# Row numbers for the edge stage's gathers: fetched by SyncE from memory instead of copied by VectorE

## The reference, cut to what matters

```python
xc = x[row]
xn = x[col]
h = relu(xc @ W1[:d] + xn @ W1[d:] + b1)
mask = sigmoid(h @ W2 + b2)[:, 0]
seg_sum = segment_sum(mask, row, num_segments=n)
w = mask / (seg_sum[row] + 1e-09)
agg = segment_sum(w[:, None] * xn, row, num_segments=n)
out_emb = where((deg > 0)[:, None], 0.5 * x + 0.5 * agg, x)
return relu(out_emb @ Wl + bl)
```

## Time and profile before

| | |
|---|---|
| median of three runs | 4384.71 us |
| the profiled execution | 4387.37 us, its span 4385.7 us |
| edge stage, first to last one-hots | 2721.3 to 4281.3 us |
| mean granted TensorE clock | 0.876 |
| busy over the span | PE 82%, DVE 73%, ACT 49%, POOL 35% |

### The profile page before, as it was taken

One profiled execution on the slowest core, in us unless ns is written; L12 is line 12 of the kernel. 1 busy time (PEld: TensorE's weight loads), 2 busy tenths in 40 slices (PEclk: granted clock), 3 DMA queues, 4 the chain that ended last, 5 costly groups with the idle time before them and its releaser, 6 DMA issues. The chain is left out here.

```text
span 4385.7 us, 95324 instructions
## 1 busy us (share of the span) xinstructions
PE 3589.6 (82%) x20539; PEld 2449.5 (56%) x20540; DVE 3189.3 (73%) x13027; ACT 2150.5 (49%) x6722; POOL 1552.8 (35%) x1256
## 2 busy tenths in 40 slices
PE   4868882798889999986997996888888888888884
PEld 2367781333333444433444445777787777777773
DVE  8899997798888888863003006888888888888885
ACT  0078893366767888862002004444444444444444
POOL 0068873000000000001011002776777777777760
PEclk8855555799999999997998998999999999999996
DMA  2011112001111222215874872444444444444451
GB/s 46 1 10 15 16 17 79 18 34 47 68 72 77 93 94 94 102 78 211 304 248 188 305 270 89 140 136 138 136 139 136 139 139 135 140 135 139 137 133 36
DMA packets 236581, 496.86 MB, mean 113 GB/s; under 512 B 52663, under 2 KB 153166, under 8 KB 236350
## 3 DMA queue, kind: packets, MB, share of 16 engines
q1 hardware_dynamic: 170017, 345.58, 23.3%
q0 software_dynamic: 66336, 149.10, 12.5%
HBM read 390.62 MB, written 103.93 MB: 113 GB/s over the span
## 5 line engine op out<-in xcount | busy, mean ns | idle before, releaser
L1676 POOL DMA_INDIRECT xs<-edge_table,ea_row_stage x1088 | 1103.6, 1014 | 463.3 <-issue 307.8
L1842 PE MATMUL ea_psa<-xs,slot_dst 128*128 128x129 f32 x3264 | 456.3, 284 | 239.7 <-DVE agg_t L1756 238.2
L1842 PEld LDWEIGHTS ea_psa<-xs,slot_dst 128*128 128x128 f32 x3264 | 413.7, 194 | 274.0 <-DVE agg_t L1756 265.5
L1231 PE MATMUL a_agg_ps<-a_adj_ring,parts 128*128 128x512 f16 (+1 forms) x2548 | 522.7, 368 | 47.6 <-DMA a_adj_ring<-adjacency 47.5
L1876 ACT ACTIVATE slot_dst<-ea_onehot,ea_mask 128x128 f32<-128x128 f16 x1632 | 535.3, 399 | 13.2
L1030 PE MATMUL ab_agg_ps<-ab_adj_stage,parts 128*128 128x512 f16 x1911 | 532.6, 389 | 0.0
L1756 DVE TENSOR_TENSOR agg_t<-agg_t,ea_psa 128x129 f32 x1632 | 462.9, 284 | 84.3 <-PE ea_psa L1842 69.3
L1870 ACT ACTIVATE ea_mask<-ea_dot,b 128x4 f32<-128x4 f32 x408 | 121.3, 297 | 807.7 <-DVE slot_src L1782 806.3
L448 ACT ACTIVATE dst_step<-iota,dst_low_bias 128x128 f16<-128x128 f16 x1188 | 358.4, 403 | 217.0 <-PEq L473 214.1
L428 POOL DMA_INDIRECT records<-both_parts,record_row x98 | 346.9, 3539 | 313.8 <-ACT both_parts L454 289.5
L1371 POOL TENSOR_TENSOR parts<-xs,parts 128x896 f16<-128x896 f32 x7 | 13.2, 1881 | 1227.9 <-ACT parts L1365 1227.9
(11 more groups left out here) (379 smaller groups left out, 6528.2 us busy)
## 6 DMA issues: line engine op xcount, KB each, us to landing
a_adj_ring<-adjacency SPq DMA_DIRECT2D x182, 896.0 KB, 4.6
ea_low_rows<-low_rows SPq DMA_DIRECT2D x411, 128.0 KB
adjacency<-ab_adj_stage SPq DMA_DIRECT2D x91, 512.0 KB, 2.6
adjacency<-ab_adj_stage SPq DMA_DIRECT2D x91, 384.0 KB, 2.3
ea_near_rows<-near_rows SPq DMA_DIRECT2D x137, 128.0 KB
xs<-edge_table,ea_row_stage POOLq DMA_INDIRECT x1088
edge_table<-vx SPq DMA_DIRECT2D x12, 512.0 KB, 2.9
records<-zero_rows SPq DMA_DIRECT2D x4, 840.0 KB, 10.2
```

The source lines that it names most:

```text
L1231: ins = nc.tensor.matmul(ps[:, h, 0:width], lhs(r, t), ring[:, g % SLOTS, k * DB:k * DB + width], start=t == 0 and r == 0, stop=t == NT - ...
L1676: nc.gpsimd.indirect_dma_start(got[:, h, g, k, 0:ROW], None, m.table, bass.IndirectOffsetOnAxis(ap=row_s[:, h, g, k:k + 1], axis=0)).then_ ...
L1842: ins = nc.tensor.matmul(psa[:, home, k, 0:AW], hot_m[:, g, k, :], what, start=True, stop=True)
```

## The change

The table of row numbers is written once to memory (`row_columns`, 128 x 1664 integers) at the head of the stage. In its step t, SyncE waits until the gathers of pass t have landed, kind by kind, and then fetches the row numbers of pass t+2 into the half of `row_s` that they have left, 128 rows of 16 bytes per kind. GpSimd waits for these DMAs instead of VectorE's copies. A plan row grows by four columns, of which 32 and 33 hold the first columns of pass t+2's far groups; two more DMAs write them in `plan_edges`. VectorE stages the rows of passes 0 and 1 alone.

```diff
@@ plan_edges
+            sp.dma_start(rows_of(0, 32, 34)[:, 0, :], plan[:, 1, 16:18]).then_inc(s_put, 16)
+            sp.dma_start(rows_of(1, 32, 34)[0:TURNS - 1, 0, :], plan[1:TURNS, 0, 16:18]).then_inc(s_put, 16)
-            sp.wait_ge(s_put, 64)
+            sp.wait_ge(s_put, 96)
@@ shared
-    m.plan = nc.dram_tensor("plan_rows", [PLAN_ROWS, 32], I32).ap()
+    m.row_cols = nc.dram_tensor("row_columns", [P, SCP], I32).ap()
+    m.plan = nc.dram_tensor("plan_rows", [PLAN_ROWS, STEP_W], I32).ap()
@@ edge_attention, gpsimd
                 for g in FAR:
-                    gp.wait_ge(s_rows, t * 2 + (g + 1))
-                    if seen >= 2:
+                    if seen < 2:
+                        gp.wait_ge(s_rows, t * 2 + (g + 1))
+                    else:
+                        gp.wait_ge(s_next[h][g], i * 16)
                         gp.wait_ge(s_agg[g], t - 1)
@@ sync
-                base = load(sp, slot, 28, 4)
+                base = load(sp, slot, 28, 6)
...
+            def fetch_next(base, h, i):
+                for g in FAR:
+                    sp.wait_ge(s_got[h][g], i * (16 * G) + 16 * G)
+                    sp.sem_inc(s_seen_sp, 1)
+                    c = nc.s_assert_within(base[g], 0, SC, ...)
+                    sp.dma_start(row_s[:, h, g, :], m.row_cols[:, bass.ds(c, G)]).then_inc(s_next[h][g], 16)
...
-                fetch_rows(1 - h, 1 - h)
+                then = fetch_rows(1 - h, 1 - h)
+                fetch_next(then, h, i)
                 sp.wait_ge(s_read, t + 1)
...
             fetch_rows(0, 0)
-            turns(sp, step)
+            sp.wait_ge(s_table, 1)
+            sp.dma_start(m.row_cols, row_of).then_inc(s_kept, 16)
+            sp.wait_ge(s_kept, 16)
+            turns(sp, step, after=after)
@@ vector
             ch(nc.vector.tensor_scalar(row_of, ai, float(NP - 1), None, ALU.min))
+            dve.sem_inc(s_table, 1)
...
                 base = v[12:15]
-                stage_rows(base, 1 - h)
                 one_hots(base, t, 1 - h, seen)
...
-            base = load(dve, 0, 28, 4)
+            base = load(dve, 0, 28, 6)
             dve.sem_inc(s_read, 1)
-            stage_rows(base, 0)
+            stage_rows(base[0:2], 0)
+            stage_rows(base[4:6], 1)
```

More of the change, by code:

```diff
@@ L36 @@
 PLAN_ROWS = 212
+STEP_W = 36
 ACT_FROM = 5
@@ L770, in plan_edges @@
         plan = sb("plan", [TURNS, 2, 19], I32)
-        none = sb("none", [P, 2 * 32], I32)
+        none = sb("none", [P, 2 * STEP_W], I32)
         psv = ctx.enter_context(nc.psum_tensor("pl_values_ps", [P, NB4, 16], F32))
@@ L1614, in edge_attention @@
         ramp = sb("ramp", [P, P, G], F16)
-        steps = sb("steps", [1, 2, 32], I32)
+        steps = sb("steps", [1, 2, STEP_W], I32)
         row_s = sb("row_stage", [P, 2, 2, G], I32)
@@ L1636, in edge_attention @@
             sem(n) for n in ("v", "ones", "rows", "near_x", "add", "seen", "seen_sp", "seen_dve", "seen_pe", "read", "read_pe"))
+        s_table, s_kept = sem("table"), sem("kept")
+        s_next = [[sem(f"next{h}{g}") for g in FAR] for h in (0, 1)]
         s_hot_t, s_u, s_z, s_dot, s_mask, s_hot, s_hot_m, s_agg = (
@@ L1691, in fetch_rows @@
                 sp.dma_start(rel[:, h, :], m.near_rows[bass.ds(c, G), :].rearrange("(o a) b -> o (a b)", o=1).broadcast_to([P, G * P])).then_inc(s_low[h], 16)
+                return base[4:6]
+            def fetch_next(base, h, i):
+                for g in FAR:
+                    sp.wait_ge(s_got[h][g], i * (16 * G) + 16 * G)
+                    sp.sem_inc(s_seen_sp, 1)
+                    c = nc.s_assert_within(base[g], 0, SC, skip_runtime_bounds_check_because="the plan holds columns")
+                    sp.dma_start(row_s[:, h, g, :], m.row_cols[:, bass.ds(c, G)]).then_inc(s_next[h][g], 16)
             def step(t, h, i, seen):
@@ L1707, in step, with after @@
                 fetch_steps(t + 2, h)
+            def after(end):
+                for h in (0, 1):
+                    for g in FAR:
+                        sp.wait_ge(s_next[h][g], end * 16)
+                        sp.sem_inc(s_seen_sp, 1)
             fetch_steps(0, 0)
```

## The result

The changed kernel takes 4377.22 us (median of 15 runs, 4369.24 to 4383.16), the kernel before 4384.94 (15 runs): a ratio of 0.9979, interval 0.9972 to 0.9986. That is 7.7 us off, where 28 were forecast: clear of the noise, but within the 0.3% that the prediction called the same. The profiled execution of the changed kernel is the fastest of its runs.

What follows compares the result with a forecast made beforehand. No engine is always busy; common passes were bound by a circle through VectorE's order including the copies, low-clock passes by TensorE. -26 - 8 + 1.7 + 4 = -28 us gave 4356 us, range 4330 to 4388.

Steps and rivals of the forecast that it cites:

- a common pass loses 0.29, one with the low clock nothing: VectorE's copies removed from the loop: 0.29 us saved in each of 89 full-clock passes, 26 us; none where TensorE's clock falls.
- Given back: Rival, chance 0.18: 46 more passes fall to TensorE's low clock (4384), or the copies only covered the sequencer (4382).
- the sequencer: At VectorE's head of a pass: the copies only covered the sequencer's work, leaving -8 + 6 = -2, 4382 us.
- The low clock goes too: Rival, chance 0.12: TensorE idles less, so its low-clock passes vanish, 0.62 us each; all 47 gone 4327, half gone 4342.
- Late gathers, -8: In the loop: GpSimd runs ahead, so VectorE's 9.5 us of waits for gathers mostly go; 8 us saved, between 0 and 11.
- Stage head, +4: At the edge stage's head: plan row 2 waits for pass 0's gathers, making TensorE 4 us late on pass 1 (0 to 7).
- Plan, +1.7: When the plan is written: two more DMAs at 0.85 us each cost 1.7 us once (0.4 to 3).
- SyncE, 0, and its DMAs: SyncE's added waits and two DMAs a pass: plan row and low rows come later but within slack, DMA engines under 70%; 0.
- SyncE rival: Rival, chance 0.14: late gathers hold SyncE's queue, so plan and low rows hold everybody; half a us a pass, +68, 4424.
- GpSimd's waits: Sign of a right forecast, in the loop: GpSimd, no longer waiting for VectorE's copies, waits for TensorE's sums instead.

Runs made afterwards that it cites:

- e1: The changed kernel with VectorE's two copies per pass put back, into a tile nobody reads: 4385.44 us, ratio 0.9995 to the kernel before.
- e3: The kernel before the change, with TensorE doing all far lookups of kind 1 twice: 4374.60 us, ratio 0.9969 to the kernel before.
- e2: The changed kernel, with TensorE doing all far lookups of kind 1 twice: 4339.95 us, ratio 0.9889 to the kernel before.
- f4: The changed kernel, with two of the four lookups of kind 1 done twice: 4334.12 us, ratio 0.9877 to the kernel before.
- h2: The kernel before the change, with two of the four lookups of kind 1 done twice: 4384.01 us, ratio 0.9994 to the kernel before.

## Why the prediction was wrong

**The step that failed: "a common pass loses 0.29, one with the low clock nothing", times 89, is 26 us.** The term measured 7 to 8 us (e1 to the changed kernel). Per pass, both halves of the sentence nearly hold. The copies gave 0.26 us in the passes without the gap (e3 to e2, 11.06 to 10.80 by the median) and about as much at a turn, less the gap's growth of 0.1. Low-clock passes stayed at 11.56. What failed is the count and the baseline, as if low-clock passes stood apart. I took the common pass as one kind of 11.27, and low-clock passes as 0.33 longer. In truth there were two kinds, 11.56 and 11.15. A low-clock pass cost nearly nothing at a turn, and 21 of 46 were there. The shorter passes moved them: now 43 stand on passes of 10.80. Their number hardly changed (46, 44), but their price went from 13 us to 37. The table adds up so: at a turn 45 passes x 0.11 and without the gap 41 x 0.35 give 19 us; 18 passes more of the short kind at the low clock take back 18 x 0.76 = 14, and 20 fewer at a turn give 20 x 0.19 = 4. With 2 for the other low-clock passes that is the 11 us between the two means. The profiled runs themselves are 18 us apart. Of the rest, 3 are in the one pass behind the 132 (15.0 us before, with a wait of 3.5 for gathers, 12.0 after).

**"Given back" (0.18)** had the right place, the low clock, and the wrong mechanism: 46 more such passes at 0.62 each. There were two fewer; each became dearer. Its other half, the sequencer, is partly right: the gap grew from 0.35 to 0.45 and 0.53, from 21.7 to 29.1 us in all. With the copies back (e1) it is 22.6. So the copies did cover some of the load, about a fifth of the 33.6 us that they took themselves.

**"The low clock goes too" (0.12)** reasoned from TensorE's idle time, which "in a common pass [...] shrinks from 2.3 to 2.0 us". It went to 2.35 and 1.72 by turns, and this shows where low-clock passes can fall. I took this idle time, ahead of the first sums of kind 1, in the first 130 passes of all fifteen traces. The 354 passes with the low clock all have 1.81 us or more of it, and the 1235 passes that have less than 1.8 are all at full clock. Before, a turn pass behind one at full clock had 1.93 and could fall; in the changed kernel it has 1.72, and one of 66 fell (it had 1.84). So only the short kind, with its 2.35, is left for them. The same tells f4 from h2: passes without the gap have 1.76 in f4 and 1.88 in h2. A long idle time isn't enough: the pass at 3444.45 follows 2.35 us and has 1.00, as have 360 others with 1.8 or more in these traces. What picks among them stays open.

The Trainium skill, TensorE: Matmul & The Clock Gate, section "Loop structure matters more than you think", has a long wait for DMA between matmuls as what makes TensorE go cold, and VectorE's copying out of PSUM as what doesn't, with the next matmuls following at once. Here they don't follow at once: TensorE's waits are for VectorE's add, 0.8 to 2.4 us in each pass, and the clock falls. Filling a part of them took the low clock away (e2, f4).

**Late gathers, -8:** right as to the wait, of which none is left in the stretch (in e3, which gathers as before, it is 12.9 us). Its worth isn't shown: everything but the copies together gave 2 us in e1, between 6 gained and 2 lost.

**Stage head, +4:** wrong. TensorE started its second pass 3.7 us later as forecast, but there was idle time to swallow it: VectorE reached its first addition of that pass no later (20.1 us behind its first one-hots, 20.5 before). **Plan, +1.7:** SyncE took 0.9 us more for the plan's DMAs; what that delayed isn't shown.

**SyncE, 0, and its DMAs:** right but for one thing. Its wait for the plan row fell to 103.7 us, nobody else is seen to wait for that row in the loop, and the packets rose by 33196 in the stretch of 1330 us (111503 to 144699) with the DMA share going from 0.47 to 0.48. The row-number DMA took 0.33 us to issue, under the 0.46 assumed. But the near rows now come late at times, as the prediction's signs for its SyncE rival have it for the low rows: VectorE waits for them once to four times in every kernel with the change, 0.5 to 5.7 us in all, and never in before, e3 and h2. It is far from a bound, but it takes back a part of what the gathers gave. GpSimd's waits did not turn to TensorE's sums (3.5 us). Its idle time is nearly the same, 375.7 us (387.1 before), most of it the 0.30 us between two gathers; longer gaps come to 1 us a pass, and for nearly all of them the trace names nothing that ended them.

## What to carry to other kernels

Sort a loop's passes by kind before multiplying a gain by a count: here a mean of 11.27 hid 11.56 and 11.15. Time taken off an engine that another waits for can move low-clock passes onto the passes just shortened, so price them by the pass they land on, not by how many there are. Where TensorE idles a couple of us in each pass, giving it useless work is a cheap test (37 and 43 us off the changed kernel; off the one before 13 and 2, the 2 within the noise). A register load at a loop's head is worth moving, once, behind an instruction long enough to cover it. And before you put a price on one engine's lag, follow it to the engine that sets the pace.

## What the runs showed that I had not expected

TensorE with 10% more work in a pass made the kernel 0.9% faster, 4377 to 4340 us. A pass in which its clock falls takes about 11.6 us in all kernels that have such passes, whether its like at full clock takes 10.80 or 11.56. A load of three registers takes more than twice as long as one of four. And cutting VectorE's load in two makes a pass 0.16 us longer than the 10.80 of one without the gap, in three another 0.16.
